# Layer 3 of a pairwise network once every four steps, on a ring of eight, with the normed tokens sent to DRAM in the first stage

## The reference, cut to what matters

```python
x = L0_attn_x                          # (16, 256, 256)
xn = _layernorm(x, axis=-1)
return x + attn(xn, ...) + ffn(xn, ...)

# attn, after a second layer norm of its own with gamma and beta:
h = einsum('bsd,fd->bsf', xn, W1)                      # 128 features
pair = relu(h[:, :, None, :] - h[:, None, :, :] + b1)  # every pair (i, j)
pair = relu(einsum('bijf,gf->bijg', pair, W2) + b2)    # layer 2: 128 -> 64
sim = einsum('bijg,og->bijo', pair, W3)[..., 0] + b3   # layer 3: 64 -> 1
# diagonal 0; each token keeps its 25 most similar tokens;
# softmax attention with 32 heads of 2 numbers over these 25; W_out; residual

# ffn: routed part and shared part
# router, 2 of 8 experts for each token, 640 slots for each expert:
buf = zeros(8, 640, 256).at[e_flat, safe_pos].set(x_flat[tok], mode='drop')
h = silu(gate) * up ; out_buf = h @ w_down ; gather, weigh, add
shared = (silu(x_flat @ gate) * (x_flat @ up)) @ shared_w_down   # 704 wide
```

## Time and profile before

| | us |
|---|---|
| three runs, median | 1682.68 |
| three runs, lowest and highest | 1680.66, 1686.21 |
| the profiled execution, its own time | 1682.04 |
| its span, first to last instruction | 1680.1 |
| PE busy, share | 1622.9, 97% |
| DVE busy, share | 1541.7, 92% |
| ACT busy, share | 1446.2, 86% |
| POOL busy, share | 1059.5, 63% |
| layer 2 on PE, 4096 records | 945.5 |
| layer 3 on PE, 2048 records | 272.8 |
| DVE's rows of layer 1, 2464 | 772.6 |
| ACT's rows of layer 1, 1632 | 729.1 |
| ACT's relus of layer 2, 512 | 590.4 |

### The profile page before, as it was taken

How to read it: one execution, slowest core, us unless ns; L and a number is a source line. 1 busy time by engine, 2 the same in 40 slices (tenths; PEclk the granted TensorE clock), 3 DMA queues, 4 the chain that set the end, 5 groups by cost and what they waited for, 6 DMA issues and landing times.

```text
span 1680.1 us, 32738 instructions
## 1 busy us (share of the span) xinstructions
PE 1622.9 (97%) x9092; PEld 707.8 (42%) x9092; DVE 1541.7 (92%) x4301; ACT 1446.2 (86%) x2674; POOL 1059.5 (63%) x1009
## 2 busy tenths in 40 slices
PE   7889999999999999999999999999999999989998
PEld 6732222222222222222222222222222999978887
DVE  6887889999999999999999999999998878878786
ACT  5689999999999999999999999999999687743342
POOL 3203567777777777777777777676677532376553
PEclk9999999999999999999999999999999999999999
DMA  5512311212212121212212111111141555433332
GB/s 161 197 57 76 103 46 47 65 49 66 64 47 67 48 64 48 66 51 62 65 48 63 47 53 50 41 45 44 42 131 38 167 174 180 161 113 98 114 110 66
DMA packets 78329, 135.88 MB, mean 81 GB/s; under 512 B 22336, under 2 KB 43712, under 8 KB 78272
## 3 DMA queue, kind: packets, MB, share of 16 engines
q0 software_dynamic: 31744, 69.27, 14.7%
q1 hardware_dynamic: 46528, 65.92, 11.8%
HBM read 91.04 MB, written 39.85 MB: 78 GB/s over the span
## 4 chain that ended last, share of the span: by engine, by line
DVE 56%; PE 26%; issue 8%; ACT 2%; DVEq 1%; DMA 0%; ACTq 0%
DVE arena L1368 29%; PE ps L883 16%; PE ps L843 7%; DVE arena L1436 5%; DVE arena L1426 3%; DVE arena L1406 3%; DVE idx L1393 3%; DVE smax L1417 2%; DVE arena L1392 2%; PE ps L854 2%; DVE top L1386 2%; DVE arena L1411 1%; DVE arena L1421 1%; ACT arena L1052 1%; PE ps L900 1%
## 5 line engine op out<-in xcount | busy, mean ns | idle before, releaser
L680 POOL DMA_INDIRECT arena<-kv_rows,gidx x800 | 843.1, 1054 | 370.1 <-issue 222.5
L843 PE MATMUL ps<-arena,w2t 128*64 128x512 f32 x4096 | 945.5, 600 | 12.1 <-DVE arena L1368 6.6
L1368 DVE TENSOR_SCALAR arena<-arena 128x256 f32<-128x256 f32 x2464 | 772.6, 372 | 20.0 <-PE ps L843 17.6
L1052 ACT ACTIVATE arena<-arena 128x256 f32<-128x256 f32 x1632 | 729.1, 552 | 12.8 <-DVE arena L1358 12.8
L1065 ACT ACTIVATE arena<-ps,b 128x1024 f32<-128x1024 f32 x512 | 590.4, 1153 | 5.2 <-PE ps L843 5.2
L843 PEld LDWEIGHTS ps<-arena,w2t 128*64 128x64 f32 x4096 | 267.4, 136 | 679.0 <-issue 511.3
L854 PE MATMUL ps<-arena,w3win 128*32 128x512 f32 x2048 | 272.8, 605 | 8.3 <-DVE arena L1378 8.3
L854 PEld LDWEIGHTS ps<-arena,w3win 128*32 128x32 f32 x2048 | 40.3, 108 | 216.3 <-issue 154.3
L648 POOL DMA_INDIRECT slot_inputs<-xstage,istage x64 | 70.1, 1096 | 96.0 <-issue 59.6
L1436 DVE TENSOR_TENSOR arena<-arena 128x1152 f32<-128x1152 f32 (+4 forms) x160 | 108.6, 678 | 0.4
L743 POOL DMA_INDIRECT arena<-slot_outputs,slot_get x64 | 68.4, 1069 | 51.9 <-PE ps L883 31.9
(11 more groups left out here) (150 smaller groups left out, 1927.2 us busy)
## 6 DMA issues: line engine op xcount, KB each, us to landing
arena<-kv_rows,gidx POOLq DMA_INDIRECT x800
slot_inputs<-arena SPq DMA_DIRECT2D x16, 640.0 KB, 3.9
arena<-slot_inputs SPq DMA_DIRECT2D x40, 256.0 KB, 3.6
slot_outputs<-arena SPq DMA_DIRECT2D x40, 256.0 KB, 2.2
arena<-in_L_attn_x_dram SPq DMA_DIRECT2D x16, 256.0 KB, 3.0
xstage<-arena SPq DMA_DIRECT2D x16, 256.0 KB
xn_rows<-arena SPq DMA_DIRECT2D x16, 256.0 KB
arena<-in_L_attn_x_dram SPq DMA_DIRECT2D x8, 512.0 KB, 4.2
```

The costliest lines, as they stand in the source:

```text
L680: pool.indirect_dma_start(out=kvg[:, h, r, :], out_offset=None, in_=kv_dram, in_offset=bass.IndirectOffsetOnAxis(ap=gidx[:, h, r:r + 1], a ...
L843: last = nc.tensor.matmul(ps_l2(s)[v * G2:(v + 1) * G2, u, :], w2t[:, :], r1[:, s % R1, 4 * u + 2 * v:4 * u + 2 * v + 2, :], start=True, s ...
L1052: last = nc.scalar.activation(r1[:, s % R1, k, :], hneg_now, ACT.Relu, bias=hb_now[:, at:at + 1])
L1368: row = nc.vector.tensor_scalar(r1[:, s % R1, k, :], hneg_now, hb_now[:, at:at + 1], 0.0, ALU.add, ALU.max)
```

## The change

Layer 3 runs after layer 2 of steps 1, 5, 9, ... (every fourth step, `L3_STEPS`), and takes two groups, four steps, each time; a batch's last four steps come at step 1 of the next batch, and after the last batch both groups stand behind the transposes of the first two slot groups. The ring `r2` has eight places in place of four, in the space of `xn1`, and the 4096 numbers it had stay empty but for `kvs` and `zeros`. For this the normed tokens have to leave `xn1` before the pair phase: the spill to `xn_dram` moves to the first stage, behind the zeros in `store_batch`, with a wait for ACT's copy of the batch. ACT's first `relu2` waits for all 16 spills. The staging tile is filled from `xn_dram`. The load of `swug`, which shares the space, waits for the last layer 3.

```diff
--- before.py
+++ after.py
@@ -62,7 +62,8 @@
     STEPS = P // STEP_ROWS
     BSTEPS = HALVES * STEPS
     R1 = 4
-    R2 = 4
+    R2 = 8
+    L3_STEPS = 4
 
 
     NPE = CAP // P
@@ -149,7 +150,7 @@
         hneg, hb = (h_both[:, k:k + 1, :].rearrange("p o n -> p (o n)") for k in range(2))
         rows_base = taken[0]
         r1 = part(R1 * STEP_ROWS * S, R1, STEP_ROWS)
-        r2 = part(R2 * 2 * 512, R2)
+        taken[0] += 4096
         attn_base = taken[0]
         kvg = part(2 * TOPK * 2 * KD, 2, TOPK)
         prod_at = taken[0]
@@ -167,6 +168,8 @@
         assert pair_end <= KEPT
         taken[0] = KEPT
         xn1 = part(NT * D, NT)
+        taken[0] = KEPT
+        r2 = part(R2 * 2 * 512, R2)
         top8 = sb("top8", [P, ROUNDS, 8])
         idx8 = sb("idx8", [P, ROUNDS, 8], u32)
         gidx = sb("gidx", [P, 2, ROUNDS * 8], u32)
@@ -490,6 +493,9 @@
 
                 sp.dma_start(zv[:, ds(b, 1), :].rearrange("p k n -> p (k n)"), zeros).then_inc(slots_zeroed, 16)
 
+                sp.wait_ge(ln_step[0], START + (b + 1) * LN[0])
+                sp.dma_start(xn_dram[:, ds(b * HALVES, HALVES), :], xn1[:, ds(b * HALVES, HALVES), :]).then_inc(xn_spilled, 16)
+
                 sp.wait_ge(qkv_saved, START + b * 2 + 2)
                 sp.dma_start(kv_dram[ds(b * S, S), :].rearrange("(h p) n -> p h n", p=P), kvs)\
                   .then_inc(kv_stored, 16)
@@ -503,12 +509,11 @@
 
 
             sp.wait_ge(route_done, 1)
-            sp.wait_ge(ln_step[0], START + NB * LN[0])
+            sp.wait_ge(xn_spilled, 16 * NB)
 
             def stage(b):
-                sp.dma_start(xstage[:, :, :], xn1[:, ds(b * HALVES, HALVES), :]).then_inc(staged, 16)
+                sp.dma_start(xstage[:, :, :], xn_dram[:, ds(b * HALVES, HALVES), :]).then_inc(staged, 16)
                 sp.dma_start(istage[:, :], slot_put[:, ds(b * (HALVES * 2), HALVES * 2)]).then_inc(staged, 16)
-                sp.dma_start(xn_dram[:, ds(b * HALVES, HALVES), :], xn1[:, ds(b * HALVES, HALVES), :]).then_inc(xn_spilled, 16)
 
             stage(0)
             with sp.Fori(1, NB) as b:
@@ -547,10 +552,8 @@
             for g in range(XE):
                 load_slots(g)
 
-            sp.wait_ge(xn_spilled, 16 * NB)
+            sp.wait_ge(l3_done, NB * GROUPS)
             sp.dma_start(swug, swug_d.rearrange("(c p) m -> p c m", p=P)).then_inc(swug_loaded, 16)
-
-            sp.wait_ge(l3_done, NB * GROUPS)
             sp.dma_start(swdn[:, 0:JC, :], swdn_d[0:JC * P, :].rearrange("(c p) d -> p c d", p=P)).then_inc(swdn_loaded, 16)
             sp.dma_start(swdn[0:KD, JC, :], woutt_d).then_inc(swdn_loaded, 16)
             sp.dma_start(swdn[KD:KD + TAIL, JC, :], swdn_d[JC * P:J, :]).then_inc(swdn_loaded, 16)
@@ -848,13 +851,14 @@
 
 
                 pe.wait_ge(r2_done, steps)
-                q = s // 2
-                at = 32 - 2 * q
-                for c in range(4):
-                    last = nc.tensor.matmul(ps[32 * c:32 * c + 32, 6, :], w3win[:, at:at + 32],
-                                            r2[:, (s - 1 + c // 2) % R2, 512 * (c % 2):512 * (c % 2) + 512],
-                                            start=(q == 0), stop=(q == GROUPS - 1))
-                last.then_inc(l3_done, 1)
+                for first in range(s, s + L3_STEPS, 2):
+                    q = first // 2
+                    at = 32 - 2 * q
+                    for c in range(4):
+                        last = nc.tensor.matmul(ps[32 * c:32 * c + 32, 6, :], w3win[:, at:at + 32],
+                                                r2[:, (first + c // 2) % R2, 512 * (c % 2):512 * (c % 2) + 512],
+                                                start=(q == 0), stop=(q == GROUPS - 1))
+                    last.then_inc(l3_done, 1)
 
             def pair_batch(b, first):
                 for s in range(BSTEPS):
@@ -865,13 +869,13 @@
 
                         pe.wait_ge(route_done, 1)
 
-                    if s == 1 and not first:
-                        layer3(b * BSTEPS, BSTEPS - 1)
-                    elif s % 2 == 1 and s > 1:
-                        if s == 3 and not first:
+                    if s % L3_STEPS == 1 and s > 1:
+                        if s == L3_STEPS + 1 and not first:
 
                             pe.wait_ge(sim_taken, b)
-                        layer3(b * BSTEPS + (s - 1), s - 2)
+                        layer3(b * BSTEPS + (s - 1), s - 1 - L3_STEPS)
+                    elif s == 1 and not first:
+                        layer3(b * BSTEPS, BSTEPS - L3_STEPS)
 
             pair_batch(0, True)
             with pe.Fori(1, NB) as b:
@@ -933,7 +937,7 @@
 
             for g in range(AHEAD):
                 transpose_slots(g)
-            layer3(NB * BSTEPS, BSTEPS - 1)
+            layer3(NB * BSTEPS, BSTEPS - L3_STEPS)
             for g in range(ALL):
                 if g + AHEAD < ALL:
                     transpose_slots(g + AHEAD)
@@ -1059,6 +1063,7 @@
 
                     act.wait_ge(slots_zeroed, 16 * NB)
                     act.wait_ge(kv_stored, START + 16 * NB)
+                    act.wait_ge(xn_spilled, 16 * NB)
                 if wait_group is not None:
 
                     act.wait_ge(l3_done, wait_group)
@@ -1079,7 +1084,7 @@
                     back = s - LAG
                     if not (first and back < 0):
                         relu2(b * BSTEPS + (back + 1), back % BSTEPS,
-                              None if first and back < R2 else b * (BSTEPS // 2) + (back // 2 - 1))
+                              None if first and back < R2 else b * (BSTEPS // 2) + (back // 2 - R2 // 2 + 1))
                     if s % STEPS == EXP_AT and done > 1:
                         exp_scores(b * HALVES + (h - 4))
 
@@ -1088,7 +1093,7 @@
             with act.Fori(2, NB) as b:
                 pair_batch(b, 2)
             for back in range(LAG, 0, -1):
-                relu2(NB * BSTEPS - back + 1, BSTEPS - back, NB * (BSTEPS // 2) - 2)
+                relu2(NB * BSTEPS - back + 1, BSTEPS - back, NB * (BSTEPS // 2) - R2 // 2)
 
 
             def gate_up_high(e):
```

## The result

The changed kernel took 1692.85 us (median of six runs, 1690.60 to 1693.45) against 1684.80 for the kernel before (six runs beside it): 1.0048 of its time, 95% interval 1.0037 to 1.0058. It is slower by 8 us. The prediction (1682.5, with 0.66 on "the same" and a range of 1675 to 1692) was wrong. The profiled execution has a span of 1691.1 us, 11.0 more than before; 3 of these are the spread of single executions.

What follows compares the result with a forecast made beforehand. DVE was taken as the limit from the third batch on, PE and ACT before. Terms -0.5 + 0 + 0.35 + 0 = -0.15 us on 1682.04 gave 1681.9, as median 1682.5; range 1675 to 1692.

Steps and rivals of the forecast that it cites:

- the same: Whole kernel: a time within 0.3% (5 us) of the kernel before, where no change can be told; chance 0.66.
- What bounds the kernel: Pair phase: from the third batch DVE is full, ACT within 0.8 us of it, PE third; first two batches: PE and ACT.
- Layer 3 in blocks of two: Pair phase: PE saves 0.17 us a block, 1.4 a batch, worth 0 us from the third batch on.
- Batches 0 and 1: First two batches: PE's saving can use ACT's idle time; -0.5 us, bounds -1.7 and +0.9.
- Transfers in the loop: Pair loop: spill gone, staging tile read from DRAM, POOL not busy enough to matter; 0 us, bounds -2 and +2.
- The shared weights: End of pair phase: later weights load, group 4's slots behind it still in time by 0.8 us; 0, bounds 0 and +4.
- rival C: After the pair phase: the slots of group 4 come late at an otherwise idle PE; +1 to +4 us, 1685; 15%.
- End of the pair phase: Both last groups run after the last step, delaying the transposes of slot group 2; +0.35 us, bounds 0 and +0.9.
- Ring place: Ring of eight where the normed tokens were: ACT's first second-layer relu also waits for their 16 transfers; 0 us.
- first stage: Before the pair phase: each of 16 batches gets one more 256 KB transfer; 0 us, bounds 0 and +11.
- Rival D: The stage before the pair phase waits for its transfer queue; up to +11 us, 1693; 5%.

Runs made afterwards that it cites:

- g1: The mended kernel: changed kernel with slots of groups 4 and 5 ahead of the shared weights and EARLY = 5; 1684.93 us, 1.0003 of the kernel before.
- h2: Kernel before with layer 3's matmuls of groups 1 to 14 narrowed from 512 to 32 columns, output not the reference's; 1.0011 of the kernel before.
- f1: The changed kernel once more, unaltered, in a disturbed session; 1.0042 of the kernel before.
- g3: Kernel before with only the normed tokens stored to DRAM in the first stage and staged from there; 1685.68 us, 1.0008 of the kernel before.
- g2: Changed kernel with five batches in place of six scattered ahead of the first gathers, nothing else; 1688.69 us, 1.0024 of the kernel before.
- g4: Kernel before with only the load of the shared gate-up weights moved behind the wait for the last layer 3; 1687.19 us, 1.0012 of the kernel before.
- h3: The changed kernel again, unaltered, in a disturbed session; 1.0027 of the kernel before.
- e2: Changed kernel with five batches in place of six scattered ahead of the first gathers, in a disturbed session; 1.0012 of the kernel before.
- f2: Changed kernel with five batches in place of six scattered ahead, in another disturbed session; 1.0022 of the kernel before.
- f4: Changed kernel with slots of groups 4 and 5 first and five batches scattered ahead, in a disturbed session; 0.9994 of the kernel before.

## Why the prediction was wrong, point by point

- **What bounds the kernel**: right for batches 2 to 14. DVE's batch kept its 75.2 us with PE's load cut by 1.4 (g1), and the batch of the disturbed runs kept its 87.8 with PE's load cut by 10% (h2).
- **Layer 3 in blocks of two**: right in size. The block of 16 records takes 1.92 us (1.93 expected), so the 0.17 us of a change of shape is paid once a block. The Trainium skill, page "TensorEngine Tiling (Array Packing)", section "Key Properties", has a drain at each change of the tiling mode; the trace agrees and puts it at those 0.17 us. ACT waited for layer 2 in 0.8 us over five times, where 0.3 in each of eleven batches was expected, and its waits for DVE's copy shrank from 9.1 to 7.8 us.
- **Batches 0 and 1, -0.5**: the size came out by luck. The rows for it, 96 to 170 us, are batch 0's, and batch 0 gained nothing (72.7 in f1 for 72.6); batch 1 gave 0.6 (72.8 in g1 for 73.4). What failed is that I priced this saving apart from the gathers. I asked for PE, ACT and DVE what else would be late, never for POOL, whose six batches of scatters stand in one queue ahead of the gathers and which a faster batch 1 only meets sooner.
- **Transfers in the loop, 0 with bounds of -2 and +2**: the step that failed for batch 1. "0.3 us more or less in each of the first six stagings" was right by itself (0.3 in g3, where the transfers stand alone). But POOL's 412 of 550 us busy, from which I took the 0, belongs to the later batches. From its first scatter to the first gather POOL is one chain of scatters and of waits for its staging tile, and the kernel before had nothing to spare at its end. This chain grew by 3.2 us in g3 and by 4.8 in the changed kernel. With 3.2 us of wait from the transfers and 4.3 from the four-step order it came to 7.5, beyond both bounds, and batch 1 lasted 3.9 us longer.
- **The shared weights, 0 "by a margin of 0.8 us"**: failed. The transfer was sized too fast, but that was the smaller part: the slots landed 1320.53 - 1310.87 = 9.7 us after the weights' issue, for 1312.5 - 1303.2 = 9.3 expected. (The 1.6 us to start and 0.7 to land in it stand in no row; only the whole was measured. The upper bound at 201 GB/s leaves out the 0.7.) What was wrong is the deadline. The transposes at 1312.92 of the earlier trace rows are those of group 5; group 4's stand at 1308.81, one row earlier in that timeline, since 1303.53 of the earlier trace rows is group 2 and groups follow at 2.6 us at first. With 1308.81 + 0.35 the same sum gives 3.3 us late, and 3.62 (after), 3.47 (g2), 3.21 (g4) were measured. So rival C was the case, with the price that its own sum gives. Behind the weights the slots took 7.50 us to land, in the median 3.6. The Trainium skill, page "DMA: Bandwidth & Descriptors", section "Queues, rings and completion order", says that each DMA engine takes descriptors in ring order. The trace agrees: the up-gate weights land 6.2 us after their issue, at 1317.1, the large part of the down weights 7.8 after theirs, at 1319.1, and the slots behind them at 1320.5.
- **End of the pair phase, +0.35**: right. From the last copy to the transposes of group 2 it is 83.6 us before and 84.1 after, 0.5 more, and they wait for DVE.
- **Ring place, first stage**: right. Rival D has 1693, which is the time measured, but by another cause. ACT, DVE and PE have the same waits between 30 and 96 us in both traces to a tenth of a us. The later start of the pair phase (0.7 us) stems from the first 20 us and stands also in g4 (97.3), which has the old first stage.
- **Batch 0**: 2.7 us of the profiled difference were no effect of the change. g4, with the old code there, took 1.7 us more in batch 0, with a granted clock of 0.75 in the mean of 98.4 to 105.2 us, and the changed kernel's batch 0 lasted 72.7 in f1, where the clock stayed at 1.00 there (72.6 before).

By place, the 11.0 us between the profiles are +0.7 (start), +2.7 (clock), +3.9 (gathers), +0.4 (13 batches) and +3.4 (slots), but for the rounding. Pieces of one span must add up; what tells the causes are the edits, by which the two waits are 4.0 and 3.5 of the 8.05 us between the medians.

No version beat the kernel before: the mended one is its equal (1.0003).

## What to carry to other kernels

A saving on an engine that does not set the pace is not neutral: it brings forward everything that waits for a third party, here indirect transfers behind a queue of others. When loads change order in a queue, take for each transfer behind them the row of its own consumer, count the groups in that timeline one by one, and ask how far ahead of its use it is issued: the slots behind 2.2 MB took 7.5 to 8.3 us to land here, so they fit only where that much is in hand. Where a cost of 0 stands on a margin of 0.8 us, the row that gives the deadline has to be checked twice.

## What the runs showed of the hardware

- Behind an idle time of PE of 3 us the granted clock fell to 0.5 (1.2 GHz) in some executions and not in others of the same code. All 20 traces have PE idle for 2.97 us ahead of batch 0. In the 7 in which batch 0's first matmul started at 98.34 to 98.85 us the clock stayed at 1.00; in the 13 in which it started at 98.95 to 99.56 it fell, the changed kernel's among the 13 and the same kernel's in f1 among the 7. In the changed kernel it was 0.50 for the 6.8 us from 98.4. That batch 0 took 2.7 us more, so a wait of PE can cost nearly twice what it lasts. Behind the 3.62 us for the slots the clock fell too (0.51 in 1320.4 to 1323.8), but there the end of the kernel came only 3.4 us later, no more than the wait.
- In four of five sessions PE stood still about twice in each batch from batch 1 on, at the same two places of the code, with some 3 to 6 us between two matmuls, and in batch 1 up to 11.2 (h3). All other engines then wait for it, and the profile finds no releaser ("remote"). The timeline of f1, the changed kernel:

```profile
343.59 1.40 DVE L1373 TENSOR_SCALAR arena<-arena 128x256 f32<-128x256 f32 x5 [2.08 <-remote]
343.68 1.11 ACT L1070 ACTIVATE arena<-ps,b 128x1024 f32<-128x1024 f32 x1 [4.56 <-remote]
...
344.85 1.97 PE L846 MATMUL ps<-arena,w2t 128*64 128x512 f32 x4 [5.23 <-ACT arena L1070]
```

  ACT waits for layer 2 of a step whose records end at 339.6; batches lasted 86 to 88 us in place of 75.2. One and the same chip showed both conditions an hour or less apart, and h2, with 10% less work on PE, had batches as long. With fewer batches scattered ahead (e2, f2, f4) the long standstill of batch 1 was absent (batch 1 took 77.4 us, with six ahead 81 to 87). Its cause stays open.
